# Two bank pairs for gate and up, and an earlier split of layer two's weights, in a two-layer attention and feed-forward kernel

## The reference

```python
x = x + xattn0(layernorm(x), ctx)        # kv = ctx W^T + b; softmax(norm(p kv kv^T))
x = x + ffn0(layernorm(x))               # dense gelu(x Wg) * (x Wu) Wd, plus top-2 of 8 experts, RMS norms
x = x + xattn1(layernorm(x), ctx, ctx)   # 16 heads of 32, 4 key heads, rotary, causal softmax, @ w_out^T
x = x + ffn1(layernorm(x))               # silu(x Wg) * (x Wu) Wd
```

## Time and profile before

| | us |
|---|---|
| median of 3 runs | 1860.8 |
| lowest, highest | 1858.88, 1864.35 |
| the profiled execution, its own time | 1861.49 |
| its span | 1859.6 |
| PE busy | 1702.2 |
| DVE busy | 1142.7 |
| ACT busy | 801.1 |
| mean granted clock of PE | 0.959 |

### The profile page before, as it was taken

The page is one execution under the profiler, slowest core; times in us unless marked ns, Lnnn a source line. Parts: engine busy times, 40 slices in busy tenths (PEclk is TensorE's granted clock), DMA queues, the critical chain, the costliest instruction groups (busy, mean ns, idle before and its releaser), DMA issues.

```text
span 1859.6 us, 27270 instructions
## 1 busy us (share of the span) xinstructions
PE 1702.2 (92%) x9460; PEld 1355.9 (73%) x9460; DVE 1142.7 (61%) x2444; ACT 801.1 (43%) x1791; POOL 238.6 (13%) x237
## 2 busy tenths in 40 slices
PE   3688997999988998799999999887999999999998
PEld 2577776888888986577667668666776778678887
DVE  5798688755565747974666665798466553543222
ACT  3565553334665742324555554442264551431111
POOL 1213226411121204210000001311000000000000
PEclk8698998999999999899999999888999999999999
DMA  3325456898798897769245327987952546245562
GB/s 104 113 103 179 155 163 244 293 351 283 251 307 309 275 338 282 269 235 304 63 141 160 86 70 267 361 322 274 310 169 61 171 130 215 80 140 195 196 215 93
DMA packets 125864, 384.87 MB, mean 207 GB/s; under 512 B 14497, under 2 KB 29217, under 8 KB 119969
## 3 DMA queue, kind: packets, MB, share of 16 engines
q1 hardware_dynamic: 118944, 360.59, 57.1%
q0 software_dynamic: 6784, 22.55, 3.5%
HBM read 278.75 MB, written 104.33 MB: 206 GB/s over the span
## 4 chain that ended last, share of the span: by engine, by line
PE 62%; DVE 17%; DMA 8%; issue 6%; ACT 4%; SPq 1%; POOL 1%; ACTq 0%; DVEq 0%; POOLq 0%
PE ps L1178 17%; PE ps L1180 16%; PE ps L1179 16%; PE ps L1332 5%; DMA raw<-in_ffn_w 4%; PE ps L1341 3%; DMA gu<-w_dram 2%; PE ps L1324 2%; PE ps L1184 2%; DVE gu L1678 2%; DVE act L1663 1%; DVE wd L1678 1%; ACT hid L1389 1%; DVE yb L1903 1%; PE ps L1325 1%
## 5 line engine op out<-in xcount | busy, mean ns | idle before, releaser
L1178 PE MATMUL ps<-xT,gu 128*128 128x512 f32 (+1 forms) x1392 | 535.2, 384 | 72.5 <-DVE act L1663 36.5
L1180 PE MATMUL ps<-xT,gu 128*128 128x512 f32 (+1 forms) x1392 | 514.6, 370 | 0.0
L1179 PE MATMUL ps<-xT,gu 128*128 128x512 f32 (+1 forms) x1392 | 514.0, 369 | 0.0
L1178 PEld LDWEIGHTS ps<-xT,gu 128*128 128x128 f32 x1392 | 271.3, 195 | 125.5 <-DVE act L1663 43.0
L1180 PEld LDWEIGHTS ps<-xT,gu 128*128 128x128 f32 x1392 | 269.8, 194 | 43.7
L1179 PEld LDWEIGHTS ps<-xT,gu 128*128 128x128 f32 x1392 | 271.2, 195 | 36.3
L1178 PE MATMUL ps<-wd,hid 128*128 128x512 f32 x604 | 249.6, 413 | 15.6 <-DVE acc L1698 9.0
L1179 PE MATMUL ps<-wd,hid 128*128 128x512 f32 x604 | 239.3, 396 | 0.0
L1180 PE MATMUL ps<-wd,hid 128*128 128x512 f32 x604 | 239.1, 396 | 0.0
L1389 ACT ACTIVATE hid<-act 128x512 fp32r<-128x512 f32 (+1 forms) x174 | 99.9, 574 | 299.6 <-DVE act L1663 298.4
L1663 DVE TENSOR_TENSOR act<-act,ps 128x512 f32<-128x512 f32 (+1 forms) x174 | 106.8, 614 | 151.1 <-PE ps L1180 150.4
(11 more groups left out here) (279 smaller groups left out, 2300.5 us busy)
## 6 DMA issues: line engine op xcount, KB each, us to landing
gu<-w_dram SPq DMA_DIRECT2D x160, 512.0 KB
raw<-in_ffn_w SPq DMA_DIRECT2D x94, 768.0 KB
wd<-w_dram SPq DMA_DIRECT2D x80, 512.0 KB, 5.4
w_dram<-gu SPq DMA_DIRECT2D x32, 1024.0 KB
w_dram<-wd SPq DMA_DIRECT2D x32, 512.0 KB
QT<-q_dram SPq DMA_DIRECT2D x48, 256.0 KB, 5.7
y_dram<-x SPq DMA_DIRECT2D x23, 512.0 KB
wcs<-tab_dram SPq DMA_DIRECT2D x16, 512.0 KB, 5.9
```

What stands on the lines that cost most here:

```text
L1178: mm(out_ap, ah, bh, start=start, stop=False)
L1179: mm(out_ap, ah, bl, start=False, stop=False)
L1180: return mm(out_ap, al, bh, start=False, stop=stop)
```

## The change

Two things.

First, tiles with an odd number use banks 4 and 5 for gate and up where no attention runs: the experts, pass 3, pass 5 and pass 8. Even tiles, and all tiles elsewhere, use banks 0 and 1 as before. The planner and all waits follow (`gate_bank`, `up_bank`).

Second, pass 5 no longer splits layer two's weights. They are split in pass 4, in 48 pieces (gate, up and down of 16 tiles), with three new kinds of steps: `eload` loads a piece (256 KB) into the memory of `raw`, which is no longer used otherwise, in three slots; `esplit` makes the high part on ACT and the low part on DVE, in place; `estore` stores both (512 KB) to `w_dram`. The first load stands behind the first tile of pass 4. Pass 5 then loads split weights like passes 6 to 8, and has no stores.

```diff
     def is_raw(s):
-        return MAIN[s][0] == "E" or MAIN[s][1:3] in ((0, 0), (0, 1), (1, 0))
+        return MAIN[s][0] == "E" or MAIN[s][1:3] in ((0, 0), (0, 1))
     def is_kept(s):
-        return MAIN[s][0] == "F" and MAIN[s][1:3] in ((0, 1), (1, 0))
+        return MAIN[s][1:3] == (0, 1) and MAIN[s][0] == "F"
+    def gate_bank(s):
+        return 4 if s % 2 and (MAIN[s][0] == "E" or MAIN[s][1:3] in ((0, 2), (1, 0), (1, 3))) else 0
+    def up_bank(s):
+        return gate_bank(s) + 1
...
+    "eload": lambda: [("estore", b - 3)] if b > 2 else [("w", LAST_EXPERT, 2)], "esplit": lambda: [("eload", b)], "estore": lambda: [("esplit", b)],
...
+        if item == ("eload", 0):
+            return [("gate0", FIRST["F", 0, 3])]
...
+    SIDES = [pieces_of("eload", 3 * HT), pieces_of("esplit", 3 * HT), pieces_of("estore", 3 * HT)]
...
+        early = raw[:, :, :, :].rearrange("p a m d -> p (a m) d").rearrange("p (r k) d -> p r k d", k=2)
...
+                elif kind == "eload":
+                    n = a[0]
+                    if n < 3:
+                        sp.wait_ge(w_low, PIECE["w", LAST_EXPERT, 2])
+                    else:
+                        sp.wait_ge(wd_stored[n % 3], early_store(n - 3))
+                    load(early[:, n % 3, 1, :], ffn_w_in[2 * HT + n // 3][:, n % 3, :]).then_inc(early_loaded[n % 3], 16)
+                elif kind == "estore":
+                    n = a[0]
+                    sp.wait_ge(early_low, n + 1)
+                    load(w_dram[1][n // 3][:, n % 3, :, :].bitcast(F32), early[:, n % 3, :, :]).then_inc(wd_stored[n % 3], 16)
...
-                return three(ps[:, m, 0:width(s)], gu[:, s % 2, m, 0, rows(d)], gu[:, s % 2, m, 1, rows(d)],
+                return three(ps[:, gate_bank(s) + m, 0:width(s)], gu[:, s % 2, m, 0, rows(d)], gu[:, s % 2, m, 1, rows(d)],
...
+                elif kind == "esplit":
+                    n = a[0]
+                    act_.wait_ge(early_loaded[n % 3], 16 * (n // 3 + 1))
+                    if n > 2:
+                        act_.wait_ge(wd_stored[n % 3], early_store(n - 3))
+                    func(early[:, n % 3, 0, :].bitcast(F32R), early[:, n % 3, 1, :], ACT.Copy).then_inc(early_high, 1)
...
+                elif kind == "esplit":
+                    n = a[0]
+                    dve.wait_ge(early_high, n + 1)
+                    piece = early[:, n % 3, :, :]
+                    tt(out=piece[:, 1, :].bitcast(F32R), in0=piece[:, 1, :], in1=piece[:, 0, :], op=ALU.subtract).then_inc(early_low, 1)
```

More of the change, by code:

```diff
@@ L278, in steps @@
             "split": [("ACT", 0.53), ("DVE", 0.6)], "project": [("PE", 2.85), ("DVE", 0.6)], "rown4": [("ACT", 0.71)], "rowt4": [("PE", 0.36), ("ACT", 0.48), ("DVE", 0.6)],
-            "rn2": [("DVE", 1.5), ("PE", 2.0), ("ACT", 0.5)]}.get(kind, [])
+            "esplit": [("ACT", 0.53), ("DVE", 0.6)], "rn2": [("DVE", 1.5), ("PE", 2.0), ("ACT", 0.5)]}.get(kind, [])
     def builds_on(item):
@@ L313, in builds_on @@
             return on
+        if kind == "gate":
+            return [("low", a[0] - 2)] if a[0] > 1 else []
         if kind in QUARTERS and kind != "up0":
@@ L539, in merge @@
         return placed, orders
-    SIDES = [[[("raw", r)] for r in range(2, len(RAW))], *([[("pre", s, m)] for s in PRE] for m in range(3)), [[("wstore", s)] for s in KEPT], [[("wostore", j)] for j in range(2)],
+    SIDES = [pieces_of("eload", 3 * HT), pieces_of("esplit", 3 * HT), pieces_of("estore", 3 * HT)]
+    SIDES += [[[("raw", r)] for r in range(2, len(RAW))], *([[("pre", s, m)] for s in PRE] for m in range(3)), [[("wstore", s)] for s in KEPT], [[("wostore", j)] for j in range(2)],
              [[("dstore", g, t)] for g in range(len(GROUPS)) for t in range(group_tiles(g))], split_ticks(), expert_ticks(), [[("xtload", b)] for b in range(1, B)]]
@@ L588, in two_layers, with early_store @@
     GU_STORES, WD_STORES = loads_of(KEPT, 2), loads_of(KEPT, 3)
+    def early_store(n):
+        return 16 * sum(1 for s in KEPT if s % 3 == n % 3) + 16 * (n // 3 + 1)
     ctx = ExitStack()
@@ L1370, in _ @@
                     W = width(s)
-                    o, z = act[:, s % 2, 0:W], ps[:, 0, 0:W]
+                    o, z = act[:, s % 2, 0:W], ps[:, gate_bank(s), 0:W]
                     act_.wait_ge(gate_done, nth("gate", s))
@@ L1648, in _ @@
                     s = a[0]
-                    o, z = act[:, s % 2, :], ps[:, 0, :]
+                    o, z = act[:, s % 2, :], ps[:, gate_bank(s), :]
                     dve.wait_ge(sq_ready, POLY[s])
@@ L1654, in _ @@
                     s = a[0]
-                    o, z = act[:, s % 2, :], ps[:, 0, :]
+                    o, z = act[:, s % 2, :], ps[:, gate_bank(s), :]
                     dve.wait_ge(tanh_ready, TANH[s])
-                    stt(out=o, in0=o, scalar=1.0, in1=z, op0=ALU.add, op1=ALU.mult).then_inc(free[0], 1)
+                    stt(out=o, in0=o, scalar=1.0, in1=z, op0=ALU.add, op1=ALU.mult).then_inc(free[gate_bank(s)], 1)
                 elif kind == "mult":
@@ L1661, in _ @@
                     dve.wait_ge(up_done, nth("up", s))
-                    dve.wait_ge(free[0], use(0, "gate", s))
-                    tt(out=act[:, s % 2, 0:W], in0=act[:, s % 2, 0:W], in1=ps[:, 1, 0:W], op=ALU.mult).then_inc(free[1], 1)
+                    dve.wait_ge(free[gate_bank(s)], use(gate_bank(s), "gate", s))
+                    tt(out=act[:, s % 2, 0:W], in0=act[:, s % 2, 0:W], in1=ps[:, up_bank(s), 0:W], op=ALU.mult).then_inc(free[up_bank(s)], 1)
                 elif kind == "low":
```

20 lines of the change are left out of this document (12 added, 8 removed).

## The result

The changed kernel is slower: its time is 1.0034 of before's, with a 95% interval of 1.0021 to 1.0046, by 13 runs of each (median 1868.5 us, 1861.5 to 1873.3, against 1861.7). That is 6 us more where 29 less were forecast. Two of e8's twelve executions, at 2119 and 3281 us, were far slower than the others and are left out of its ratio.

What follows compares the result with a forecast made beforehand. Only PE's idle time and slow clock could be won, with DVE nearly the bound in the middle of passes 3 and 5. Terms -3 - 11 - 18 - 7 + 10 = -29 took 1861.5 to 1832.5 us, range 1798 to 1856.

Steps and rivals of the forecast that it cites:

- the rivals: Three alternatives: DVE isn't the bound (chance 0.18, 1796 us); banks give nothing (0.15, 1848); pass 4 pays (0.10, 1888).
- The second rival: Experts and pass 3: banks give nothing because everything waits for DVE's queue; -13 in total, 1848 us; chance 0.15.
- Pass 3, -11: Pass 3, second bank pair: 7 of 9.3 idle us between 720 and 814 won, plus 4 of lag.
- the 4 us of lag: Pass 3: PE leaves the middle stretch up to one tile (5.4 us) ahead, of which 4 us counted.
- Pass 5, -18: Pass 5, 1180 to 1270: without 16.7 us of splits, DVE's remaining work needs 72 of 90 us.
- -7 around it: Rest of pass 5 and start of pass 6: idle time and slow clock won, -7 us.
- Pass 4, +10: Pass 4, where the splits go: 6 us for engine work and 4 for queued transfers.
- The engines' 6 us: Pass 4: ACT's copies and DVE's subtractions cost 0.13 us for each of 48 pieces, 6 us.
- 8 us, of which I count 4 on the path: Pass 4: three loads and three stores (2.36 MB) ahead of gate weights take 8 us, 4 counted.
- The ring: Pass 4's three piece slots: 2.8 us a piece, 4.0 at worse figures, against 4.3 available, so it holds.
- Experts, -3: Experts, second bank pair: the 3.1 us wait for `act` L1663 can go, -3 us.
- three signs of being wrong: Pass 3's `act` waits gone unreplaced; pass 3 within 2 us of 161; pass 4 over 310 with ACT idle before copies.

Runs made afterwards that it cites:

- e8: The late start (e3) planned with one pair of banks instead of two; ratio 1.0052 to the kernel before.
- e7: The changed kernel without one DVE instruction of the final step, order the same; ratio 0.9962 to the kernel before.
- e13: The kernel before with its own order on every engine, but two bank pairs in use; ratio 1.0002 to the kernel before.
- e3: The late start: the changed kernel with the first piece's load behind pass 4's fifth tile, not its first; ratio 0.9921 to the kernel before, 1842.5 us.
- e14: The order of e3 on every engine, with one bank pair in use instead of two; ratio 0.9978 to the kernel before.
- e5: The changed kernel with the gathers opening batch 2's work between the layers held behind tile 115; ratio 0.9966 to the kernel before.
- e11: The changed kernel with two planner costs set as measured (DVE's parts 2.1, qrow 1.5 us), work unchanged; ratio 0.9986 to the kernel before.
- e17: The changed kernel with the turns of query rows planned two us later, work unchanged; ratio 0.9977 to the kernel before.
- e4: The changed kernel without ACT's copy and DVE's subtraction of the 48 pieces, loads and stores kept; ratio 0.9991 to the kernel before, 1859.0 us.
- e1: The kernel before with the second pair of banks alone; ratio 0.9958 to the kernel before, 1851.6 us.
- e2: The changed kernel with one pair of banks, so the moved splits alone; ratio 1.0010 to the kernel before, 1863.0 us.
- e9: The changed kernel with batch 1's work between the layers held to tile 90; ratio 1.0115 to the kernel before.
- e12: The late start (e3) with batch 3's work between the layers held to tile 122; ratio 0.9975 to the kernel before.
- e15: The late start (e3) joined with the two corrected planner costs of e11; ratio 0.9942 to the kernel before.
- e18: The late start (e3) with the turns of query rows planned two us later; ratio 0.9949 to the kernel before.

## Why the prediction was wrong

The sign was wrong, and none of the rivals was what happened, though the second came near it in pass 3. Point by point:

**Pass 3, -11, measured -3.4.** The reading of the bound was right: DVE was nearly the bound (0.90 of the stretch before, 0.92 after), and e7 shows it, with 7.9 us for 6 us of work. The step that failed is "of its 9.3 idle us I take 7 as won", with the 4 us of lag. The idle time was not won: the waits for `act` became waits for `hid`, `qb` and the accumulation, and PE's idle time stayed at 23.8 us. The second rival ("the banks give nothing") described this, and in the order of before it holds within 3 us (e13, 1.0002). The Trainium skill's sentence on a kernel that gained nothing from a second PSUM buffer (TensorE: Matmul & The Clock Gate, section "HAM oscillation — how this bites in real kernels") is borne out by e13, and e3 against e14 shows its limit: with another order the same banks gave 11 us.

**Pass 5, -18, and -7 around it; measured -6.6 for both.** This is the term that turned the sum. Its step was: "66.3 of its 83.0 us are left. At its present busy share of 0.92 they need 72 us". The splits did leave, and no wait for them is left. But the step held two things fixed that the new order moved. First the other work: between tiles 118 and 126, 15.0 us of splits left and 5.8 us of mid work came in, so DVE has 8.4 us less and not 16.7. The mid work begins in tile 114 as before, stands closer, and attention of batch 2 starts at tile 128 instead of 130. That gains little, since passes 6 and 7 had no idle time to be filled. Second the share: DVE was busy 0.91 of that stretch and is busy 0.83, so 82.5 us take 99.1, where at 0.91 they would take 91. The largest waits of PE there are for turns that stand too early: 9.3 us of `qb` for the 2.1 of the earlier trace rows, a row that the prediction read and gave no term. e5, e11 and e17, which only move this order, bring the share back to 0.90 and more, and each gave 9 to 13 us.

**Pass 4, +10, measured +19.7.** The engines' 6 us were about right (e4: 8). What failed is the rest: "8 us, of which I count 4 on the path", where e4 leaves 11.4. The idle time up to tile 98 rose by 4.1 us, as sized; the clock added 7.4 us of loss, with 17 us at 1.2 GHz. The prediction had no clock term for pass 4, because the earlier trace rows showed 1.00 there. A further 5.9 us of idle time and 1.7 of slow clock came from tiles 98 to 112; e4 has nearly as much there (5.7 and 1.7). The ring held: a piece's load landed in 4.5 us and its store in 5.3 (medians), so with copy and subtraction 3.7 us a piece of the 4.3. ACT did wait 10.5 us for pieces (the row above), but no wait of PE names them.

**Experts, -3,** measured -2.1 up to tile 78. The loss there is 19.4 us before and 20.5 after, so the banks did nothing in the experts. The 2 us lie ahead of them, in passes 1 and 2, which keep banks and order: that is the variation of one execution to the next.

**The sum itself.** It added parts at a fixed order. e1 and e2 give -8 and +2 us, the whole +6: 12 us are in neither. Among the kernels of the 18 experiments, those with the whole work of the changed kernel and another order (e3, e5, e9 to e12, e15, e17, e18) lie from 0.9921 to 1.0134, 40 us apart, which is more than every term of the sum. In such a kernel the chances that I gave (0.85 faster) were far too sure.

None of the prediction's three signs of being wrong was met (pass 3 is 158 us long, pass 4 is 294), so they would not have named the cause: none of them looked at the order.

What stays open: why the clock fell at the start of pass 4 in the changed kernel and stayed up in the kernel before, with equally full DMA engines (the wait for the queries is 2.4 us in the one and 0.4 in the other, and no run changes that wait alone); how much of pass 5's low share of DVE is the turns'; and whether a plan made for the order directly would beat the late start, whose 15 us are found and not designed.

## What to carry to other kernels

Where a planner or a scheduler sets the order, predict the order's change first, from its listing: look for work that moves into the freed room, and for an in-order engine's instruction that now stands sooner than its input can be there. Price a freed resource only if what moves into it is worth something; and when parts tried alone don't add up to the whole, run the old order with the new resource and the new order without it, which separates the two in two kernels. Compare stretches of the same main-line work, not of the same length in time: the same busy share in 90 us hid that DVE had less to do and did it more slowly. What a second pair of banks is worth can't be read from the name of the wait: it gave 0, 7 and 11 us in three orders.

## What the runs showed of the hardware

Some DVE instructions are slower beside GpSimd. The same instruction `yb` of L1948 takes 0.74 us alone and 1.75 beside GpSimd's sum (rows of 1250.49 and 1251.82 above; the sum runs from 1251.32 to 1253.03); in the whole trace 8 of its 16 take 1.75 to 1.78 us, and just these begin while such a sum has 1.2 us left. The product of L1977 takes 1.37 us (alone 0.69) beside the sum that started at 1253.65 (to 1254.91). The subtraction `qtl` of L1986, which reads a bank, isn't slowed: the five that begin while a sum runs take 0.68 to 0.69 us, as the others. The Trainium skill says (SBUF — State Buffer, section "Terms") that the two share a pair of ports, which one of them holds for a whole instruction while the other stands still; the rows of `yb` and L1977 agree in kind, since DVE's instruction is longer by 1.0 us where the sum still runs 1.2, and by 0.7 where it still runs 0.8; those of `qtl` show that it doesn't hold for every DVE instruction. It matters here because the planner counts the shorter time.

Longer waits did not go with more time at the slow clock here. In the changed kernel the waits around 865 us were 2.4 and 0.9 us long and were followed by 17 us at 1.2 GHz (granted 0.53 from 866 to 884, with PE busy 15.0 of the 18 us), while the waits of 6.9 and 5.2 us in the middle of pass 3 went with a mean clock of 0.93 over the 94 us in which they lie, which is two stretches of 6.8 us at 1.2 GHz. Why is not shown.
